# A Mamba-style mixer with a postnorm mixture layer on one core: per-bank waits, a split first expert input, an unrolled batch loop and a reordered start

## The chip, the cores and the metric

The kernel runs on one core of a Trainium2 chip. The metric is the device time of one execution in microseconds (us), median of several runs. Engines are named as in the profile: PE (matmul) and PEld (its weight loads), DVE, ACT, POOL, and SP, which only issues DMAs.

## The reference

For each of 16 sequences of 512 tokens with 128 features, one layer:

```python
# mixer (8 heads of 64, state 64)
z = x @ Wz;  ssm_in = x @ Win                    # 128 -> 256, 128 -> B, C, dt, X
delta = softplus(dt_raw + dt_bias)
h = exp(delta * -exp(A_log)) * h + X_t * delta * B_t ;  y_t = h @ C_t     # scan over time
y = y + D_param * X
out = (y * (silu(z) @ Wzg)) @ Wout
x = layernorm(x + out)
# mixture: three top-3-of-12 routers dw1, dw2, dw3 from x @ P_w.T @ U.T
h = gelu(sum_e dw1[:, e] * (x @ W1[e].T))        # 128 -> 512
y = sum_e dw2[:, e] * (h @ W2[e].T) + dw3 @ b2   # 512 -> 128
x = layernorm(x + y)
```

All data are float32. Matmuls over large operands are done as three products of a rounded high part and a low part (`mm3`, lines 229 to 231).

## The kernel before

**Tiling.** One batch is one sequence, held as 4 chunks of 128 tokens. All weights stay on chip, each as a high (`_hi`) and a low (`_lo`) part. PSUM has two banks for the mixer (`mix_bank`), four for the mixture (`exp_bank`, `hb[0..3]` in the code), one shared (`turn_bank`) and one with ones on the diagonal (`unit_bank`).

**Order of the work.** There is no scheduler: each engine runs its own instruction stream, all written by the same Python functions in one order, and semaphores (`wait`, `sig`) join them. `mixer_alone` sets up the weights, does the mixer of batch 0 and the front of batch 1's. Then comes `body` for batch b: it interleaves the mixer of b (PE: scores, `mix_zg`, `mix_states`, `mix_y`, `mix_out`) with the mixture of batch p = b-1 (`expert_in` for 12 experts, `expert_gelu`, `expert_out` for 4 chunks by 3 groups), and, near its end, starts the front of the next batch (`mix_x`, `mix_bc`, `mix_dt`, `mix_step`, `mix_z`, `mix_X`). `body` is written out for batch 1, is a hardware loop (`Fori`) over batches 2 to 14, and is written out again for 15. `mixture_alone` ends the program with the mixture of batch 15. In the loop every wait whose count depends on the batch is computed in a register.

**The first expert.** `expert_row` (L1021, DVE) multiplies the transposed input by a row of router weights into `fbuf`; `expert_split` rounds it on ACT into a slot of `sp_hi` (L1036), and POOL writes the remainder to `sp_lo` (L1039). The slots of `sp_hi` and `sp_lo` that expert 0 takes are, for the batch before, gelu outputs that `expert_out` reads until its last group. The four banks that expert 0 fills are the ones that DVE empties in the last four groups of `expert_out` (L1126, and L1129 adds the two accumulators). The code of the wait before is

```python
if e == 0:
    wait(PE, "comb", b.prev())
wait(PE, "xw_lo", b, e + 1)
```

**The gate and the step size.** `mix_z` computes z on PE, tanh on ACT (L599), and finishes silu on DVE (L602); its two results lie in the banks that `mix_X` needs next. `mix_step` is the softplus chain for delta: 16 small POOL operations (L530 to L557), with an exp (L517) and a log (L519) on ACT and a reciprocal on DVE (L522). Tanh and log are in different ACT tables, so that each change is an ACT_TABLE_LOAD.

**The start.** `split_w` makes the two parts of the weight tiles, k = 0 to 15 in a ring of four stages in `fbuf`, k = 16 to 23 from other buffers; the high part is made on ACT (L408), the low part on POOL or, for the k in `LO_V`, on DVE (L412). `load_w` on SP loads a stage again once its low part is done. For heads h, ACT scales the scores (L771), DVE adds the skip (L780) and scans the decay (L791), POOL multiplies both (L798, `Wt`), and PE forms y of a pair of heads (L816, L824). The router's path is x1 transposed (L919), logits (L932), twelve maxima and the rest of `route_weights` on DVE (L952 to L976), one transpose (L990), and two trips through DRAM that spread the rows.

## Time and profile before

| | us |
|---|---|
| median of 3 runs (range) | 1641.73 (1641.39 to 1641.86) |
| the profiled execution | 1642.74 |
| its span | 1641.0 |
| PE busy | 1565.2 (95%) |
| DVE busy | 1135.9 (69%) |
| ACT busy | 592.5 (36%) |
| POOL busy | 648.8 (40%) |
| granted TensorE clock, mean of the span | 0.982 |

The span is the profiled execution as its trace shows it; its own time is 1.74 us longer, for what lies around the trace. Busy times are sums over instructions; a busy engine is not thereby the one that sets the end. In a row of the timeline the first number is the start from the beginning of the span, the second the duration, both in us; the bracket at the end says how long the engine had been idle before it, and what ended that.

### The profile page before, as it was taken

The numbers are of one execution on the slowest core, as the hardware profiler recorded it, in microseconds if no ns is written. First come the engines' busy times: TensorE is split into PE (matmuls) and PEld (weight loads), VectorE is DVE, ScalarE is ACT, GpSimd is POOL, SyncE is SP. The second block draws the span as 40 slices with busy tenths as digits, with TensorE's granted clock in tenths as the row PEclk, the third lists the DMA queues.
The fourth block names the chain that finished last, engine by engine and source line by source line (L and its number), as shares of the span: only waits on it lengthen the run. The fifth ranks groups of instructions, "written<-read, shape, count | busy, mean of one in ns | idle before, by whom it ended". The sixth has DMA issues, their size and how long they took to land.

```text
span 1641.0 us, 28331 instructions
## 1 busy us (share of the span) xinstructions
PE 1565.2 (95%) x8466; PEld 1244.5 (76%) x8466; DVE 1135.9 (69%) x3110; ACT 592.5 (36%) x1339; POOL 648.8 (40%) x740
## 2 busy tenths in 40 slices
PE   6579999999999999999999999999999999999997
PEld 4457878787787878778787777877778787787776
DVE  6457677766867767677776768677687776767744
ACT  5443342424424243342424424242342414334130
POOL 4565260623516153351624526063351614435040
PEclk9679999999999999999999999999999999999999
DMA  4332140312304032140302304031130402213020
GB/s 139 113 100 75 38 119 27 104 45 63 93 27 129 13 95 67 44 112 20 120 29 68 88 27 128 17 105 53 55 100 25 131 13 82 80 45 112 19 67 7
DMA packets 81839, 114.63 MB, mean 70 GB/s; under 512 B 10176, under 2 KB 37328, under 8 KB 81744
## 3 DMA queue, kind: packets, MB, share of 16 engines
q1 hardware_dynamic: 81744, 113.71, 23.5%
q14 instruction: 78, 0.64, 0.2%
q8 instruction: 17, 0.28, 0.1%
HBM read 108.55 MB, written 5.13 MB: 69 GB/s over the span
## 4 chain that ended last, share of the span: by engine, by line
PE 75%; issue 8%; POOL 7%; DVE 5%; ACT 3%; DMA 1%; POOLq 0%; SPq 0%; DVEq 0%; ACTq 0%
PE exp_bank L229 19%; PE exp_bank L231 18%; PE exp_bank L230 18%; PE mix_bank L816 4%; PE mix_bank L842 4%; PE mix_bank L824 3%; POOL sp_lo L1039 3%; PE mix_bank L229 2%; PE mix_bank L231 2%; PE mix_bank L230 2%; ACT L515 1%; PE turn_bank L1087 1%; DVE Xd L626 1%; POOL Wt L798 1%; PE mix_bank L932 1%
## 5 line engine op out<-in xcount | busy, mean ns | idle before, releaser
L1039 POOL TENSOR_TENSOR sp_lo<-fbuf,sp_hi 128x512 fp32r<-128x512 f32 x192 | 247.6, 1290 | 260.8 <-ACT sp_hi L1036 246.4
L229 PE MATMUL exp_bank<-sp_hi,w_hi 128*128 128x512 f32 x768 | 311.8, 406 | 17.8 <-DVE acc L1129 15.0
L229 PE MATMUL exp_bank<-w_hi,sp_hi 128*128 128x512 f32 x768 | 309.7, 403 | 2.0 <-POOL sp_lo L1080 2.0
L231 PE MATMUL exp_bank<-sp_hi,w_lo 128*128 128x512 f32 x768 | 303.8, 396 | 0.0
L231 PE MATMUL exp_bank<-w_hi,sp_lo 128*128 128x512 f32 x768 | 303.3, 395 | 0.0
L230 PE MATMUL exp_bank<-w_lo,sp_hi 128*128 128x512 f32 x768 | 303.2, 395 | 0.0
L230 PE MATMUL exp_bank<-sp_lo,w_hi 128*128 128x512 f32 x768 | 302.1, 393 | 0.0
L1036 ACT CAST sp_hi<-fbuf 128x512 fp32r<-128x512 f32 x192 | 119.0, 620 | 373.9 <-DVE fbuf L1021 304.1
L1126 DVE SCALAR_TENSOR_TENSOR acc<-exp_bank,dw,acc 128x128 f32<-128x128 f32 x384 | 131.2, 342 | 126.9 <-PE exp_bank L231 126.0
L229 PEld LDWEIGHTS exp_bank<-sp_hi,w_hi 128*128 128x128 f32 x768 | 144.9, 189 | 68.2 <-POOL sp_lo L1039 22.5
L798 POOL TENSOR_TENSOR Wt<-Wt,Gh 128x512 f32<-128x512 f32 x128 | 175.4, 1370 | 11.3 <-DVE Wt L791 11.2
L530 POOL TENSOR_TENSOR delta<-delta,bias_b 128x32 f32<-128x32 f32 x16 | 4.3, 268 | 436.5 <-ACT delta L507 436.5
L229 PEld LDWEIGHTS exp_bank<-w_hi,sp_hi 128*128 128x128 f32 x768 | 144.3, 188 | 35.3 <-issue 2.0
L231 PEld LDWEIGHTS exp_bank<-w_hi,sp_lo 128*128 128x128 f32 x768 | 144.1, 188 | 35.0
L231 PEld LDWEIGHTS exp_bank<-sp_hi,w_lo 128*128 128x128 f32 x768 | 145.1, 189 | 32.1
L771 ACT ACTIVATE Gh<-Gm,delta 128x128 f32<-128x128 f32 x512 | 163.5, 390 | 15.9 <-POOL Wt L798 11.7
L230 PEld LDWEIGHTS exp_bank<-w_lo,sp_hi 128*128 128x128 f32 x768 | 144.4, 188 | 31.7
L230 PEld LDWEIGHTS exp_bank<-sp_lo,w_hi 128*128 128x128 f32 x768 | 145.1, 189 | 29.4
L791 DVE TENSOR_TENSOR_SCAN Wt<-seg_b,unit_bank 128x512 f32<-128x512 f32 x128 | 154.2, 1205 | 0.4 <-DMA seg_b<-dA_rows 0.4
L1021 DVE TENSOR_TENSOR fbuf<-turn_bank,row_b 128x512 f32<-128x512 f32 x192 | 129.7, 677 | 28.0 <-DMA row_b<-dw_rows 25.3
L1126 DVE SCALAR_TENSOR_TENSOR acc_odd<-exp_bank,dw,acc_odd 128x128 f32<-128x128 f32 x320 | 109.4, 342 | 1.5
L780 DVE SCALAR_TENSOR_TENSOR Gh<-unit_bank,d_b,Gh 128x512 f32<-128x512 f32 x128 | 94.4, 738 | 9.6 <-ACT Gh L771 9.6
(198 smaller groups left out, 2229.1 us busy)
## 6 DMA issues: line engine op xcount, KB each, us to landing
row_b<-dw_rows SPq DMA_DIRECT2D x192, 256.0 KB, 3.4
seg_b<-dA_rows SPq DMA_DIRECT2D x128, 256.0 KB, 3.7
ctd<-cum_rows SPq DMA_DIRECT2D x128, 96.0 KB, 3.4
x_in<-in_x SPq DMA_DIRECT2D x16, 256.0 KB, 2.8
result<-acc SPq DMA_DIRECT2D x16, 256.0 KB, 2.3
fbuf<-in_W1T SPq DMA_DIRECT2D x12, 256.0 KB, 3.4
fbuf<-in_W2T SPq DMA_DIRECT2D x4, 256.0 KB, 2.7
Gh<-in_W2T SPq DMA_DIRECT2D x4, 256.0 KB, 3.5
```

The source lines that it names most:

```text
L229: nc.tensor.matmul(ps, s_hi, m_hi, start=start and j == 0, stop=False)
L230: nc.tensor.matmul(ps, s_hi, m_lo, start=False, stop=False)
L231: last = nc.tensor.matmul(ps, s_lo, m_hi, start=False, stop=stop and j == n - 1)
L771: last = AC.activation(G[:, c, :], Gm[:, c, :], ACT.Copy, scale=delta[:, c, h:h + 1])
L780: sig("G_skip", DVE.scalar_tensor_tensor(flat, unit[:, :], d_b[:, h:h + 1], flat, ALU.mult, ALU.add))
L791: sig("scan", DVE.tensor_tensor_scan(W, seg_b[h % 2][:, :], unit[:, :], 0.0, ALU.mult, ALU.add))
L798: sig("W", PO.tensor_tensor(W, W, Gh[h % 2][:, :, :].rearrange("p c t -> p (c t)"), ALU.mult))
L816: PE.matmul(ps[j * HD:(j + 1) * HD, tok(c)], Xd[:, c, h * HD:(h + 1) * HD], Wt[:, q % 2, at:at + P], start=(c == 0), stop=False)
L1021: sig("xw", DVE.tensor_tensor(wide[e % 2], rb[:, :], row_b[e % 2][:, :], ALU.mult))
L1036: sig("xw_hi", AC.copy(sp_hi[:, at, :], wide[e % 2]))
L1039: sig("xw_lo", PO.tensor_tensor(sp_lo[:, at, :], wide[e % 2], sp_hi[:, at, :].bitcast(F32), ALU.subtract))
L1126: sig("comb", DVE.scalar_tensor_tensor(dst, ps, w, dst, ALU.mult, ALU.add))
```

## The change

1. `expert_in`: expert 0 waits, bank by bank, for the group of `expert_out` that used this bank, and not for all of the batch before.
2. `expert_split` for expert 0 works in two pieces: tokens of chunks 0 to 2 (384 columns) once the groups of chunks 0 to 2 of `expert_out` are through, and chunk 3 (128 columns) after the last group. The first piece is issued at the end of the body, with `expert_row` ahead of it, and the second at the start of the next one.
3. At the end of the body `mix_step` stands ahead of `mix_z`, without a table load of its own; the load for exp and log follows the two tanh.
4. The loop is gone: `body` is written out for batches 2 to 14, so that all waits are against constants.
5. The start: `setup_zg` is taken apart, its ACT part after `mix_dt`, its DVE part after the first silu split; `LO_V` is (0, 1), so that tiles 3 and 5 have their low part on POOL; the splits of tiles 2 to 15 are spread otherwise; `mix_from_start` follows `mix_decay`; the front of batch 1 is interleaved with the router in another order, with its `Xd` copies on ACT and not DVE.

```diff
             xw=E, xw_hi=E + 1, xw_lo=E + 1, ps_h=E - 1, ...
-        N1, NHP, LO_V = 16, 2, (0, 1, 3, 5)
+        N1, NHP, LO_V = 16, 2, (0, 1)
...
-        def expert_split(eng, b, e):
+        def expert_split(eng, b, e, parts=(0, 1)):
             at = (e + 2) % NH
-            if eng is AC:
-                wait(AC, "xw", b, e + 1)
-                wait(AC, "ps_y", b.prev())
...
+            early = slice(0, (NC - 1) * P)
+            pieces = ((1, early), (2, tok(NC - 1))) if e == 0 else ((e + 2, slice(0, T)),)
+            for k, (n, cols) in enumerate(pieces):
+                if k not in parts:
+                    continue
+                if eng is AC:
+                    wait(AC, "xw", b, e + 1)
+                    wait(AC, "ps_y", b.prev(), (NC - 1) * NG if cols == early else None)
...
+                    sig("xw_hi", AC.copy(sp_hi[:, at, cols], wide[e % 2][:, cols]))
...
         def expert_in(eng, b, e):
-                if e == 0:
-                    wait(PE, "comb", b.prev())
-                wait(PE, "xw_lo", b, e + 1)
+                wait(PE, "xw_lo", b, e + 2)
                 for hc in range(NH):
+                    if e == 0:
+                        m = NC * NG - NH + hc
+                        wait(PE, "comb", b.prev(), m // NG * (E + 1) + (m % NG + 1) * EG)
...
         def body(eng, b, front_next, norm_before=True):
             if norm_before:
-                expert_split(eng, p, 0)
+                expert_split(eng, p, 0, [1])
...
             if front_next:
+                mix_step(eng, nxt, table=False)
                 mix_z(eng, nxt)
-                mix_step(eng, nxt)
+                if eng is AC:
+                    AC.preload_act_table_set(LOG_EXP)
+            expert_row(eng, b, 0)
+            expert_split(eng, b, 0, [0])
             expert_out(eng, p, 3, range(1, NG - 1))
-            expert_row(eng, b, 0)
...
         def mixer_alone(eng, b):
-            setup_zg(eng)
+            setup_masks(eng)
             mix_bc(eng, b)
             mix_dt(eng, b)
+            if eng is AC:
+                setup_zg(eng)
...
             mix_silu_split(eng, b, on=DVE)
+            if eng is DVE:
+                setup_zg(eng)
...
-            split_w(eng, range(2, 6))
             router_product(eng)
             mix_states(eng, b)
+            split_w(eng, range(2, 4))
             mix_decay(eng, b, 0)
             mix_decay(eng, b, 1)
+            split_w(eng, [4])
             mix_zg(eng, b, range(0, 2))
             mix_score_step(eng, b, 2)
             mix_zg(eng, b, range(2, 4))
-            split_w(eng, range(6, 8))
+            mix_from_start(eng, b, 0)
...
-                split_w(eng, [k])
-                k += 1
+                split_w(eng, [k, k + 1])
+                k += 2
...
             route_transpose(eng, b)
+            mix_step(eng, nxt)
+            mix_z(eng, nxt)
             route_logits(eng, b)
+            mix_silu_split(eng, nxt)
+            mix_X(eng, nxt, [0, 1], on=AC)
+            route_weights(eng, b)
+            mix_scores(eng, nxt)
+            if eng is not SP:
+                mix_rates(eng, nxt)
+            if eng in (PE, AC):
+                mix_ends(eng, nxt)
+            mix_X(eng, nxt, [2], on=AC)
             split_w(eng, range(N1, N1 + LATE))
+            if eng is PO:
+                mix_ends(eng, nxt)
+            route_rows(eng, b)
...
         def program(eng):
-            waited[id(eng)] = {}
-            with eng.Fori(2, NB - 1) as i:
-                body(eng, Batch(i, 0), True)
-            waited[id(eng)] = {}
+            for i in range(2, NB - 1):
+                body(eng, Batch(None, i), True)
```

ACT at the end of a pass of the loop and the start of the next, before. L507 is the copy of dt_raw, L599 tanh, L515, L517 and L519 the table load, exp and log of the step size; L1388 is the loop, and the row behind it is the first of the pass.

```order
L507 COPY delta<-mix_bank 128x32
L203 REGISTER_ALU
L599 ACT_TABLE_LOAD
L599 ACTIVATE Wt<-mix_bank 128x512
L203 REGISTER_ALU
L599 ACTIVATE Wt<-mix_bank 128x512
L515 ACT_TABLE_LOAD
L203 ISA
L517 ACTIVATE dt_s<-dt_s 128x32
L203 REGISTER_ALU
L519 ACTIVATE dt_s<-dt_s 128x32
L1388 COMPARE_AND_BRANCH
```

And in the change, where L602 is tanh, L1261 the table load behind it, and L1051 the two pieces of the first expert's input.

```order
L510 COPY delta<-mix_bank 128x32
L520 ACTIVATE dt_s<-dt_s 128x32
L522 ACTIVATE dt_s<-dt_s 128x32
L602 ACT_TABLE_LOAD
L602 ACTIVATE Wt<-mix_bank 128x512 x2
L1261 ACT_TABLE_LOAD
L1051 CAST sp_hi<-fbuf 128x384
L1051 CAST sp_hi<-fbuf 128x128
L704 COPY Gm<-mix_bank 128x512
```

Exp and log come first, tanh behind them and behind a table load; the number of table loads is the same, and the branch and register rows are gone.

POOL in the mixer of batch 0, before. L726 is the last work ahead of the heads, L412 the low part of a weight tile, L798 the product of a head.

```order
L726 TENSOR_TENSOR Wt<-Xd,ends 128x512 x3
L412 TENSOR_TENSOR w1_lo<-fbuf,w1_hi 128x512 x2
L798 TENSOR_TENSOR Wt<-Wt,Gh0 128x512
L798 TENSOR_TENSOR Wt<-Wt,Gh1 128x512
L412 TENSOR_TENSOR w1_lo<-fbuf,w1_hi 128x512 x2
L798 TENSOR_TENSOR Wt<-Wt,Gh0 128x512
L412 TENSOR_TENSOR w1_lo<-fbuf,w1_hi 128x512
L798 TENSOR_TENSOR Wt<-Wt,Gh1 128x512
```

And in the change, with L735, L415 and L807 for the same.

```order
L735 TENSOR_TENSOR Wt<-Xd,ends 128x512 x3
L415 TENSOR_TENSOR w1_lo<-fbuf,w1_hi 128x512 x2
L807 TENSOR_TENSOR Wt<-Wt,Gh0 128x512
L807 TENSOR_TENSOR Wt<-Wt,Gh1 128x512
L415 TENSOR_TENSOR w1_lo<-fbuf,w1_hi 128x512
L807 TENSOR_TENSOR Wt<-Wt,Gh0 128x512
L415 TENSOR_TENSOR w1_lo<-fbuf,w1_hi 128x512 x2
L807 TENSOR_TENSOR Wt<-Wt,Gh1 128x512
```

The product of head 2 has one tile ahead of it and not two, that of head 3 two and not one.

PE in the front of batch 1, before: z (its last product), then the transpose of the router weights (L990), then X0, X1 and the scores.

```order
L231 MATMUL mix_bank<-xT_hi,wz_lo 128x512
L990 MATMUL exp_bank<-ident,dwpad 128x128
L229 MATMUL mix_bank<-wx_hi,xT_hi 128x512
L230 MATMUL mix_bank<-wx_lo,xT_hi 128x512
L231 MATMUL mix_bank<-wx_hi,xT_lo 128x512
```

And in the change: the transpose (L999) stands behind X0, X1, the scores, the rates and X2, right ahead of the gate's product.

```order
L714 MATMUL mix_bank<-a_rows,upper 128x32
L229 MATMUL mix_bank<-wx_hi,xT_hi 128x512
L230 MATMUL mix_bank<-wx_lo,xT_hi 128x512
L231 MATMUL mix_bank<-wx_hi,xT_lo 128x512
L999 MATMUL exp_bank<-ident,dwpad 128x128
L229 MATMUL mix_bank<-sp_hi,wzg_hi 128x512
```

## Rows read from the trace of the kernel before

**Rows 1.** The page, its first part: busy us (share of span) and instructions.

```profile
PE 1565.2 (95%) x8466; PEld 1244.5 (76%) x8466; DVE 1135.9 (69%) x3110; ACT 592.5 (36%) x1339; POOL 648.8 (40%) x740
```

**Rows 2.** The timeline of PE: the first expert's first matmul in four batches.

```profile
199.24 0.50 PE L229 MATMUL exp_bank<-sp_hi,w_hi 128*128 128x512 f32 x1 [0.91 <-DVE acc L1129]
...
295.96 0.49 PE L229 MATMUL exp_bank<-sp_hi,w_hi 128*128 128x512 f32 x1 [0.92 <-DVE acc L1129]
...
1468.29 0.51 PE L229 MATMUL exp_bank<-sp_hi,w_hi 128*128 128x512 f32 x1 [0.90 <-DVE acc L1129]
...
1560.08 0.50 PE L229 MATMUL exp_bank<-sp_hi,w_hi 128*128 128x512 f32 x1 [2.25 <-DVE acc L1129]
```

**Rows 3.** The timeline of DVE and PE: after entering the loop, and after a jump.

```profile
199.90 0.82 DVE L658 TENSOR_TENSOR_SCAN cum_t<-dA_t,upper 32x128 f32<-32x128 f32 x1 [0.79 <-ACT dA_t L654]
...
591.76 1.27 DVE L658 TENSOR_TENSOR_SCAN cum_t<-dA_t,upper 32x128 f32<-32x128 f32 x1 [3.09 <-DMA dA_rows<-dA_t]
...
594.26 0.51 PE L229 MATMUL mix_bank<-sp_hi,wzg_hi 128*128 128x512 f32 x1 [0.34 <-DVE Xd L626]
```

**Rows 4.** DMA queues of 107 to 296 us: packets, MB, share of 16 engines.

```profile
q8 instruction: 8, 0.13, 0.3%
```

**Rows 5.** The timeline around the start of a pass, ACT, POOL, DVE and PE.

```profile
586.56 0.62 ACT L1036 CAST sp_hi<-fbuf 128x512 fp32r<-128x512 f32 x1 [4.12 <-PE exp_bank L231]
...
587.25 1.27 POOL L1039 TENSOR_TENSOR sp_lo<-fbuf,sp_hi 128x512 fp32r<-128x512 f32 x1 [0.16 <-ACT sp_hi L1036]
...
587.81 0.86 DVE L1129 TENSOR_TENSOR acc<-acc,acc_odd 128x128 f32<-128x128 f32 x1
...
588.80 0.50 PE L229 MATMUL exp_bank<-sp_hi,w_hi 128*128 128x512 f32 x1 [0.92 <-DVE acc L1129]
```

**Rows 6.** The timeline of ACT: a copy of 128 columns.

```profile
1160.19 0.27 ACT L995 COPY rows<-mix_bank 128x128 f32<-128x128 f32 x1 [3.52 <-PE mix_bank L990]
```

**Rows 7.** The timeline of the step size and the gate, in the order of starts.

```profile
578.12 0.25 POOL L535 TENSOR_TENSOR dt_s<-dt_s,delta 128x32 f32<-128x32 f32 x1
...
578.88 1.30 ACT L599 ACTIVATE Wt<-mix_bank 128x512 f32<-128x512 f32 x2 [0.84 <-PE mix_bank L231]
...
579.51 1.39 DVE L602 SCALAR_TENSOR_TENSOR Wt<-Wt,mix_bank 128x512 f32<-128x512 f32 x2
...
580.20 1.28 ACT L515 ACT_TABLE_LOAD   x1
...
581.49 0.23 ACT L517 ACTIVATE dt_s<-dt_s 128x32 f32<-128x32 f32 x1
...
582.17 0.40 PE L229 MATMUL mix_bank<-wx_hi,xT_hi 128*128 128x512 f32 x1
...
582.21 0.23 ACT L519 ACTIVATE dt_s<-dt_s 128x32 f32<-128x32 f32 x1 [0.49 <-POOL dt_s L539]
```

**Rows 8.** The timeline of the start, DVE, PE and POOL, batch 0.

```profile
26.68 3.49 DVE L412 TENSOR_TENSOR w_lo<-fbuf,w_hi 128x512 fp32r<-128x512 f32 x2 [0.28 <-ACT w_hi L408]
...
31.67 0.47 PE L229 MATMUL mix_bank<-sp_hi,wzg_hi 128*128 128x512 f32 x1 [4.26 <-DVE S L759]
...
40.22 2.56 POOL L412 TENSOR_TENSOR w_lo<-fbuf,w_hi 128x512 fp32r<-128x512 f32 x2 [3.67 <-ACT w_hi L408]
...
61.23 1.98 PE L816 MATMUL mix_bank<-Wt,Xd 128*64 128x128 f32 x16 [3.71 <-POOL Wt L798]
```

**Rows 9.** The timeline of DVE and PE: front of batch 1; then PE near the end.

```profile
83.63 0.97 DVE L952 MAX8 fbuf<-fbuf 128x8 f32<-128x12 f32 x12 [1.37 <-ACT fbuf L939]
...
92.93 0.45 PE L990 MATMUL exp_bank<-ident,dwpad 128*128 128x128 f32 x1 [7.00 <-issue]
...
99.17 0.39 PE L229 MATMUL mix_bank<-sp_hi,wzg_hi 128*128 128x512 f32 x1
...
107.22 0.50 PE L229 MATMUL exp_bank<-sp_hi,w_hi 128*128 128x512 f32 x1
...
1561.67 0.63 PE L229 MATMUL exp_bank<-sp_hi,w_hi 128*128 128x512 f32 x1
```

More of the change, by code:

```diff
@@ L329, in setup_z, with setup_masks @@
                 PE.wait_ge(sems["wbdt"], 2)
[L331 to L334 removed]
+        def setup_masks(eng):
             if eng is DVE:
@@ L340, in setup_zg @@
                 DVE.tensor_copy(unit[:, :], ident4[:, :]).then_inc(sems["cast"], 1)
+                DVE.wait_ge(sems["decay_par"], 48)
+        def setup_zg(eng):
+            if eng is AC:
+                AC.wait_ge(sems["wzg"], 16)
+                AC.activation(wzg_hi[:, :, :], st_wzg, ACT.Copy, scale=0.5).then_inc(sems["wzg_hi"], 1)
+            if eng is DVE:
                 DVE.wait_ge(sems["wzg_hi"], 1)
@@ L615, in mix_silu_split, with mix_X @@
                                                     ALU.subtract))
-        def mix_X(eng, b, cs):
+        def mix_X(eng, b, cs, on=DVE):
             for c in cs:
@@ L622, in mix_X @@
                     sig("ps_X", mm3(ps[:, :], [(xT_hi[:, tok(c)], xT_lo[:, tok(c)], wx_hi[:, :], wx_lo[:, :])]))
-                if eng is DVE:
-                    wait(DVE, "ps_X", b, c + 1)
-                    wait(DVE, "ps_yq", b.prev())
-                    sig("Xd", DVE.tensor_copy(Xd[:, c, :], bank_of(f"X{c}")[:, :]))
+                if eng is on:
+                    wait(on, "ps_X", b, c + 1)
+                    wait(on, "ps_yq", b.prev())
+                    sig("Xd", (AC.copy if on is AC else DVE.tensor_copy)(Xd[:, c, :], bank_of(f"X{c}")[:, :]))
         def mix_zg(eng, b, ns=range(NQ)):
@@ L642, in layer_program, with mix_rates @@
         R1 = slice(0, H * NC)
-        def mix_rates(eng, b):
+        def mix_rates(eng, b, start=True):
             if eng is PE:
@@ L669, in mix_rates, with start_rows @@
                 seg_row(b, 1)
+                if start:
+                    start_rows(eng, b)
+        def start_rows(eng, b):
+            if eng is SP:
                 start_row(b, 0)
@@ L1018, in expert_row @@
                 if e >= 2:
-                    wait(DVE, "xw_hi", b, e - 1)
-                    wait(DVE, "xw_lo", b, e - 1)
+                    wait(DVE, "xw_hi", b, e)
+                    wait(DVE, "xw_lo", b, e)
                 sig("xw", DVE.tensor_tensor(wide[e % 2], rb[:, :], row_b[e % 2][:, :], ALU.mult))
@@ L1024, in expert_row @@
                 expert_weight(b, e + 2)
-        def expert_split(eng, b, e):
+        def expert_split(eng, b, e, parts=(0, 1)):
             at = (e + 2) % NH
-            if eng is AC:
-                wait(AC, "xw", b, e + 1)
-                wait(AC, "ps_y", b.prev())
-                if e >= 4:
-                    wait(AC, "ps_h", b, e - 3)
-                elif e >= 2 and (b.reg is not None or b.off < NB - 1):
-                    wait(AC, "ps_zg", Batch(b.reg, b.off + 1))
-                sig("xw_hi", AC.copy(sp_hi[:, at, :], wide[e % 2]))
-            if eng is PO:
-                wait(PO, "xw_hi", b, e + 1)
-                sig("xw_lo", PO.tensor_tensor(sp_lo[:, at, :], wide[e % 2], sp_hi[:, at, :].bitcast(F32), ALU.subtract))
+            early = slice(0, (NC - 1) * P)
[6 more added lines that the diff above has]
+                    wait(AC, "ps_y", b.prev(), (NC - 1) * NG if cols == early else None)
+                    if e >= 4:
+                        wait(AC, "ps_h", b, e - 3)
+                    elif e >= 2 and (b.reg is not None or b.off < NB - 1):
+                        wait(AC, "ps_zg", Batch(b.reg, b.off + 1))
+                    sig("xw_hi", AC.copy(sp_hi[:, at, cols], wide[e % 2][:, cols]))
+                if eng is PO:
+                    wait(PO, "xw_hi", b, n)
+                    sig("xw_lo", PO.tensor_tensor(sp_lo[:, at, cols], wide[e % 2][:, cols],
+                                                  sp_hi[:, at, cols].bitcast(F32), ALU.subtract))
         def expert_in(eng, b, e):
@@ L1263, in mixer_alone @@
             mix_silu_split(eng, b, on=DVE)
+            if eng is DVE:
+                setup_zg(eng)
             if eng is AC:
```

44 lines of the change are left out of this document (14 added, 30 removed).

## The prediction

> **What bounds the kernel now.** I read the page first: PE is busy 95% of the span [rows 1]. The timeline of PE then says where the missing 5% is. From the first expert of batch 1 to the end it streams: in the middle of the program 128x512 matmuls follow each other without a gap, and only two idle rows return in every pass: about 0.9 us before the first expert [rows 2] and about 0.35 us before the gate's product [rows 3]. The reader should see in both that PE is the bound of the steady part, so that a microsecond taken from PE's waits there is a microsecond of the total, and that work of other engines counts only through these waits. The first 107 us are different: PE waits for POOL, DVE and the router for many microseconds [rows 8, 9]. So I cost four places: the jump, the boundary of the batches, the last boundary, and the start.
>
> **The jump of the loop (12 times).** Batch 2 enters the loop without a jump; the next 12 passes come after one. From first expert to first expert, batch 2 takes 295.96 - 199.24 = 96.72 us, and the 12 later passes (1468.29 - 295.96) / 12 = 97.69 us [rows 2]. The code is the same. What differs is seen on DVE: at a jump its first instruction comes 3.09 us after the one before, and without it 0.79 us [rows 3]. The profile puts those 3.09 us down to a DMA, but nothing in the code makes this scan wait for it, and it happens exactly where there is a jump; I take it to be the fetch of code behind the branch. The late scan makes the copy of X2 late, and PE waits 0.34 us for it [rows 3]; the rest of the 0.97 us comes later in the pass, through expert inputs that are late by the same cause. Unrolled, all passes should run as batch 2: -12 x 0.97 = **-11.7 us**. The registers cost nothing that I can see: batch 2 computes them too, and DVE, ACT and POOL have slack. Bounds: 0 if the fetch stall is not the jump's, and the full 11.7.
>
> The Trainium skill (Runtime: NRT & Kernel Launch, Instruction fetch mechanics) says that prefetch of code is sequential, and that a taken branch outside the current window forces a fetch before execution goes on. The 3.09 against 0.79 us agree with it.
>
> The price of unrolling is more code to fetch. In 107 to 296 us, nearly all straight code, the queue that carries PE's code moved 8 packets [rows 4], about 4 per batch, and those matmuls ran with no gap beyond those named. I charge nothing.
>
> **The boundary (14 times).** Now PE goes on at 588.80, having been idle for 0.92 us, so it was free at 587.88 [rows 5]. Two chains end together: POOL's low part at 587.25 + 1.27 = 588.52, and DVE's last add at 587.81 + 0.86 = 588.67. The change removes the second: bank 0 was emptied long before, and the last bank needs the last multiply, which ends before the add at 587.81 starts, while PE comes to it nine matmuls after its start. It shortens the first: behind the last group ACT and POOL handle 128 columns and not 512. For ACT the nearest row is a 128x128 copy, 0.27 us [rows 6]. For POOL, 128x32 takes 0.25 and 128x512 takes 1.27 [rows 5, 7]; linear between them is 0.46. Chain: 586.56 + 0.27 + 0.07 (587.25 against the end of ACT's piece) + 0.46 = 587.36, plus 0.13 (588.67 to 588.80) = 587.49, ahead of PE's 587.88. So the whole 0.92 goes. Even with POOL at 0.85 us, the wait is gone. The 384-column piece runs while PE works on the last two groups; DVE makes its row before the combines of the second-last group, which it did before those of the last one until now.
>
> What is late next? First, the gate. Exp and log now go first: POOL's fourth step ends at 578.37 [rows 7], exp can start at about 578.4, log starts 0.72 after exp as now (582.21 against 581.49) and takes 0.23, so ACT is free at about 579.35. Table load 1.28, tanh 0.65 each (1.30 for two): the first ends at 581.3, silu (1.39 for two, so 0.7) at 582.0. X0 needs that bank at 582.17, and its weights 0.23 earlier. I charge 0.15 us. Second, the gate's low part on POOL does not move with the boundary, since ACT makes the high part behind the scores: zg comes 0.92 earlier and should wait about 0.1. So the boundary gives 0.92 - 0.25 = 0.67 us, 14 times: **-9.4 us**. Bounds: 0 if another wait takes the place, 0.92 x 14 = -12.9 at most.
>
> Here a rule speaks against the change. The row says that exp starts 0.01 us after the load of 1.28 us has ended [rows 7], so that a change of tables costs 1.28. The Trainium skill (ScalarE: Activation LUTs, What ACT_TABLE_LOAD costs) adds a drain of about 1380 ns, 2.66 us in all. By it tanh would be 1.38 us later, and X0 would stall for some 1.5 us in every pass, so that the boundary would lose 0.6 us and not gain 0.67. The row shows no drain; I go by the row.
>
> **The last boundary (once).** PE was idle for 2.25 us before 1560.08 [rows 2], with ACT, POOL at full width and DVE behind each other. The short chain saves 0.35 + 0.81 us, and the add is not waited for: -1.2. Behind this gap eight matmuls ran at the lower clock (1.2 GHz; 0.63 us each, the first at 1561.67 [rows 9], against 0.40), each some 0.2 us longer from start to start; behind the 14 gaps of 0.92 none did. With a gap of about 1.1 the clock should stay up: -1.6. Together **-2.8 us** (bounds -1.2 and -2.8).
>
> **The start (once).** I followed the order by hand with the durations of the trace. Against: PE's rates wait for the low part of Wzg, which DVE now makes behind the silu split, some 1.2 us later than PE is ready. For: DVE loses two weight tiles of 3.49 us that stood ahead of the states, for which PE waited 4.26 us at the gate [rows 8]; net the gate starts some 1.7 us earlier. Then PE waits ahead of each later pair of heads for POOL's products, at the last for 3.71 us [rows 8]. POOL had two tiles, 2.56 us, ahead of head 2 [rows 8], and SP loaded rows behind waits for such tiles. With one tile ahead of head 2 and two ahead of heads 3, 5 and 7 I get the products of heads 3, 5 and 7 ready at about 43.6, 49.3 and 55.9, and y3 at 56 and not 61.2: -5.2. POOL has two tiles more, which end near 62, in time for the first expert weights. In the front of batch 1, PE stood for 7.00 us before the transposed router weights at 92.93 [rows 9], with X0 to X2 behind it until 99.17, 5.7 us of work. Those now go first; but DVE makes silu ahead of the maxima, which puts the maxima 1.6 us later than 83.63 (I get 85.2), and part of the gate's product will run at the lower clock, 1.5 us: -5.7 + 1.6 + 1.5 = -2.6. What batch 1 waits for behind its first expert stays. Start: **-7.8 us**, bounds -2 and -12.
>
> **Sum.** -11.7 - 9.4 - 2.8 - 7.8 = -31.7. The profiled execution took 1642.74 (span 1641.0), which gives 1611.0; it stood 1.0 us above the median of the runs, so I predict 1610 us.
>
> **The rivals.**
> - *Tanh is late.* A drain, or a later log, and every pass waits at X0. For it: the chain above has under 0.2 us to spare. Against: the load row. With 1.3 us more in 14 passes: 1610 + 18 = 1628. Chance 0.07.
> - *The start gives nothing.* My hand order leaves out queues of DMAs and has POOL fuller than before. Then 1618. For it: POOL's two more tiles and the late Wzg; against: the waits of 7.00 and 3.71 us [rows 8, 9]. Chance 0.12.
> - *The boundary doesn't move.* The change does not do what it says there: another wait, for the piece on POOL behind a slow ACT, takes the place of the one removed: 1610 + 9 = 1619. Against it are the 0.4 us to spare. Chance 0.08.
> - *Code does not arrive (slower).* Unrolled, PE fetches about 4 blocks in each of 12 more batches, 50 in all, and on the other engines the stream never repeats. If each block stalled PE for the 2.3 us that DVE lost at a jump (3.09 - 0.79), that is +115, less the gain of 32: 1725. It decides from 32 / 50 = 0.65 us per block on. Against it: batch 2 fetched the same way without a gap [rows 4]. Chance 0.02.
>
> **How the numbers follow.** The forecast has 0.71. Its own range is the sum's with the start between -2 and -12 and the boundary between 0.3 and 0.9 us: about 1603 to 1620. Taking in the first three rivals gives 1601 to 1625. Faster by over 0.2% (3.3 us, about what a measurement of this kernel tells from no change) holds in all cases but the last: 0.97, the same 0.01, slower 0.02.
>
> **What would show it.** Right: DVE's scan at every boundary idle for about 0.8 us; no idle row before the gate's product; the first expert with no wait, or under 0.2; pass after pass of 95.9 to 96.2 us between first experts; the first expert of batch 1 at about 99.4 and not 107.2. Wrong: an idle row before X0 with DVE's silu as its releaser (the gate is late), "issue" rows of PE at irregular places (code), or y3 still at 61 us. If passes are 95.2 us, the charge of 0.25 was too much.

## The result, and the profile after

The changed kernel takes 1606.59 us (median of 4 runs, 1604.72 to 1607.62), the kernel before on the same chip 1641.8. The ratio is 0.9783 with a 95% interval of 0.9766 to 0.98: 2.2% faster. I had predicted 1610 us with a range of 1601 to 1625, so the time lies 3.4 us below the forecast and within its range. Three of the four terms that make the sum were too small, though, and one of them for a reason that the prediction did not see. The four together were to give 31.7 us; the spans of the two profiled executions differ by 37.1. That the median lies closer to the forecast is in part luck: the profiled execution before was 1.0 us above its median, for which I allowed, and the one after is 0.55 us below its own.

| | before | after |
|---|---|---|
| median us | 1641.8 | 1606.59 |
| profiled execution, its span | 1642.74, 1641.0 | 1606.04, 1603.9 |
| first expert of batch 1 starts | 107.22 | 98.39 |
| from there to the last boundary but one (1468.29, 1433.93) | 1361.07 | 1335.54 |
| from there to the end | 172.71 | 169.97 |
| a pass in the middle, mean | 97.69 | 95.74 |

The three stretches give 8.83 + 25.53 + 2.74 = 37.1 us, the difference of the spans. The page of the profile after shows in its first part, its queues and the chain of work that ended last (by engine):

```profile
PE 1556.4 (97%) x8466; PEld 1242.3 (77%) x8466; DVE 1098.5 (68%) x3104; ACT 596.9 (37%) x1359; POOL 653.5 (41%) x758
...
q8 instruction: 67, 1.10, 0.3%
q14 instruction: 59, 0.48, 0.1%
...
PE 94%; POOL 2%; ACT 1%; DVE 1%; DMA 1%; issue 1%; SPq 0%; POOLq 0%; ACTq 0%; DVEq 0%
```

PE has 9 us less of busy time than in [rows 1], but its share rose to 97%. The unrolled program fetches PE's code in 67 packets (queue q8), where the kernel before needed 17, and no "issue" row of PE stands behind the first expert of batch 1. The other queue with code (q14) has 59 packets where the loop had 78. The timeline of PE, which answers to [rows 2], shows that the boundary has lost its idle row:

```profile
98.39 0.47 PE L229 MATMUL exp_bank<-sp_hi,w_hi 128*128 128x512 f32 x1 [0.99 <-POOL sp_lo L1054]
...
189.30 0.48 PE L229 MATMUL exp_bank<-sp_hi,w_hi 128*128 128x512 f32 x1
...
285.01 0.48 PE L229 MATMUL exp_bank<-sp_hi,w_hi 128*128 128x512 f32 x1
...
380.49 0.39 PE L714 MATMUL mix_bank<-a_rows,upper 128*128 128x32 f32 x2
380.71 0.48 PE L229 MATMUL exp_bank<-sp_hi,w_hi 128*128 128x512 f32 x1
...
1524.54 0.50 PE L229 MATMUL exp_bank<-sp_hi,w_hi 128*128 128x512 f32 x1 [0.92 <-POOL sp_lo L1054]
```

The pair of short matmuls before the first expert (L714) now starts 0.22 us ahead of it, two steps of 0.11 us with no idle time; before it was 1.30 us. The last boundary waits 0.92 us and not 2.25. The timeline of ACT, POOL and DVE around that boundary, which answers to [rows 5]:

```profile
376.19 0.52 ACT L1051 CAST sp_hi<-fbuf 128x384 fp32r<-128x384 f32 x1 [0.17 <-DVE fbuf L1030]
...
379.55 0.30 ACT L1051 CAST sp_hi<-fbuf 128x128 fp32r<-128x128 f32 x1 [2.84 <-PE exp_bank L231]
...
376.88 1.02 POOL L1054 TENSOR_TENSOR sp_lo<-fbuf,sp_hi 128x384 fp32r<-128x384 f32 x1
...
379.92 0.46 POOL L1054 TENSOR_TENSOR sp_lo<-fbuf,sp_hi 128x128 fp32r<-128x128 f32 x1 [2.03 <-ACT sp_hi L1051]
...
380.71 0.29 DVE L1146 TENSOR_TENSOR acc<-acc,acc_odd 128x128 f32<-128x128 f32 x1
382.31 0.89 DVE L661 TENSOR_TENSOR_SCAN cum_t<-dA_t,upper 32x128 f32<-32x128 f32 x1 [1.31 <-ACT dA_t L657]
```

POOL's last piece takes 0.46 us, as estimated. The surprise is DVE's add: 0.29 us, where the same instruction took 0.86 in [rows 5]. What differs is that POOL was in its 1.27 us instruction then, and now rests (its last piece ended at 380.38). And ACT with DVE and PE ahead of it, which answers to [rows 7]:

```profile
372.10 0.23 ACT L522 ACTIVATE dt_s<-dt_s 128x32 f32<-128x32 f32 x1 [0.49 <-POOL dt_s L542]
372.34 1.28 ACT L602 ACT_TABLE_LOAD   x1
373.64 1.09 ACT L602 ACTIVATE Wt<-mix_bank 128x512 f32<-128x512 f32 x2
...
374.27 1.29 DVE L605 SCALAR_TENSOR_TENSOR Wt<-Wt,mix_bank 128x512 f32<-128x512 f32 x2 [0.52 <-ACT Wt L602]
...
375.15 0.39 PE L229 MATMUL mix_bank<-wx_hi,xT_hi 128*128 128x512 f32 x1
```

The load takes 1.28 us and tanh starts 0.02 us behind its end; X0 (the last row) follows with no idle time. By the rule of the Trainium skill (ScalarE: Activation LUTs, What ACT_TABLE_LOAD costs) a drain would have come on top; the trace shows none in this place.

### The profile page after: what moved, and what is told of

Read it like the earlier page. It is cut to its first block, busy times and chain, and to the rows that moved or that the text cites. A ratio compares the mean times of both kernels' runs of the same rounds, so it can differ in the third digit from the quotient of the medians.

```text
span 1603.9 us, 24955 instructions
## 1 busy us (share of the span) xinstructions
PE 1556.4 (97%) x8466; PEld 1242.3 (77%) x8466; DVE 1098.5 (68%) x3104; ACT 596.9 (37%) x1359; POOL 653.5 (41%) x758
## 4 chain that ended last, share of the span: by engine, by line
PE 94%; POOL 2%; ACT 1%; DVE 1%; DMA 1%; issue 1%; SPq 0%; POOLq 0%; ACTq 0%; DVEq 0%
PE exp_bank L229 23%; PE exp_bank L231 22%; PE exp_bank L230 22%; PE mix_bank L825 4%; PE mix_bank L851 4%; PE mix_bank L229 4%; PE mix_bank L231 3%; PE mix_bank L230 3%; PE mix_bank L833 3%; PE mix_bank L751 1%; PE mix_bank L699 1%; PE turn_bank L1104 1%; POOL w_lo L415 1%; PE mix_bank L941 1%; PE mix_bank L500 1%
## 5 line engine op out<-in xcount | busy, mean ns | idle before, releaser
L1054 POOL TENSOR_TENSOR sp_lo<-fbuf,sp_hi 128x512 fp32r<-128x512 f32 (+2 forms) x208 | 249.6, 1204 | 258.6 <-ACT sp_hi L1051 140.5
L229 PE MATMUL exp_bank<-sp_hi,w_hi 128*128 128x512 f32 x768 | 308.5, 402 | 4.4 <-POOL sp_lo L1054 4.4
L1051 ACT CAST sp_hi<-fbuf 128x512 fp32r<-128x512 f32 (+2 forms) x208 | 121.9, 588 | 311.6 <-DVE fbuf L1030 269.6
L807 POOL TENSOR_TENSOR Wt<-Wt,Gh 128x512 f32<-128x512 f32 x128 | 175.8, 1374 | 6.9 <-DVE Wt L800 6.7
L231 PEld LDWEIGHTS exp_bank<-sp_hi,w_lo 128*128 128x128 f32 x768 | 144.6, 188 | 30.9
L230 PEld LDWEIGHTS exp_bank<-sp_lo,w_hi 128*128 128x128 f32 x768 | 144.8, 189 | 30.3
```

The source lines that it names most:

```text
L229: nc.tensor.matmul(ps, s_hi, m_hi, start=start and j == 0, stop=False)
L230: nc.tensor.matmul(ps, s_hi, m_lo, start=False, stop=False)
L231: last = nc.tensor.matmul(ps, s_lo, m_hi, start=False, stop=stop and j == n - 1)
L807: sig("W", PO.tensor_tensor(W, W, Gh[h % 2][:, :, :].rearrange("p c t -> p (c t)"), ALU.mult))
L1051: sig("xw_hi", AC.copy(sp_hi[:, at, cols], wide[e % 2][:, cols]))
L1054: sig("xw_lo", PO.tensor_tensor(sp_lo[:, at, cols], wide[e % 2][:, cols], sp_hi[:, at, cols].bitcast(F32), ALU.subtract))
```

## The experiments

Each kernel ran beside the kernel before on the same chip. The difference to the changed kernel is given by the ratios to the kernel before, times 1641.7; an interval of a ratio is 0.0013 to 0.0017 to each side, 2 to 3 us, and that of a difference of two ratios is wider. "Pass" is the mean from first expert to first expert in the profiled run, over the 13 passes from the second boundary to the last but one (with the loop restored, the 12 behind a jump). "Gap" is the start of the first expert less that of the pair of matmuls before it (L714 in the changed kernel), in a pass of the middle.

| kernel | median us | ratio | against after | pass | gap |
|---|---|---|---|---|---|
| the changed kernel again | 1605.25 | 0.9783 | 0 | 95.74 | 0.22 |
| loop restored | 1613.8 | 0.9829 | +7.6 | 96.56 | 0.22 |
| one wait for all banks | 1607.62 | 0.9795 | +2.0 | 95.91 | 0.56 |
| input in one piece | 1617.43 | 0.9848 | +10.7 | 96.48 | 1.13 |
| gate first | 1614.33 | 0.9836 | +8.7 | 96.33 | 1.00 |
| old start | 1615.17 | 0.9841 | +9.5 | 95.72 | 0.22 |
| old first routing only | 1609.55 | 0.9792 | +1.5 | 95.71 | 0.22 |
| load on POOL | 1609.31 | 0.9802 | +3.1 | 95.75 | 0.22 |
| before, loop written out | 1627.76 | 0.992 | (-13.1 to before) | 96.58 | 1.28 |
| silu rounded first | 1604.77 | 0.9762 | -3.4 | 95.56 | 0.22 |
| one tile later | 1604.81 | 0.9771 | -2.0 | 95.73 | 0.22 |
| both | 1601.75 | 0.9755 | -4.6 | 95.53 | 0.22 |

**The changed kernel again.**

> The changed kernel once more, as the base of the runs beside it: 1606.6 us within 1.5, if the result is repeatable. The rows to compare with: DVE's first addition at the first expert 0.29 us, passes of 95.7 us, DVE's scan at the turn of the batch idle for 1.31 us for its input from ScalarE.

It gave 1605.25 us (1604.09 to 1607.94) at the same ratio, with the same passes. Its runs spread over nearly 4 us, and the traces of kernels with the same start show where: the last wait for POOL's product (y3) ends at 55.1 to 59.0 us in them, with the granted clock at its lower level in other stretches each time, while the middle repeats to some 0.2 us a pass. A second place is the pass of batch 1. In most traces the clock is at its lower level once more for 3.4 us, between 108 and 125 us, and from the first expert of batch 1 to that of batch 2 it is 90.9 to 93.5 us; in three (one wait, load on POOL, both) it is not, and it is 89.2 to 89.7 us. So the start can't be read from one trace to better than 1 to 2 us.

**The loop.**

```diff
-            for i in range(2, NB - 1):
-                body(eng, Batch(None, i), True)
+            with eng.Fori(2, NB - 1) as i:
+                body(eng, Batch(i, 0), True)
```

> Only the loop is restored: 12 passes jump back again, all else is the changed kernel. Theory (each jump costs about 0.97 us on DVE's way to PE): 11.7 us slower, about 1618.3 us, each pass from the second to the last 96.7 instead of 95.7 us, and the idle time ahead of DVE's scan back at about 3 us. Rival (the time came off the boundary alone, and the jump was covered): within 1 us of the changed kernel. A second rival (code written out costs something that the jump saved, as more packets of the instruction queues): faster than the changed kernel.

By the medians 8.6 us slower, by the ratios 7.6; the spans of the two traces differ by 11.0. So the jump costs time as I said, and somewhat less behind the new boundary (12 x 0.82 = 9.8 us by the passes). Against the straight kernel, PE loses it at two places of a pass, in batch 4's for one: at the gate's product 5 us into it (0.39 us) and at an expert input 22 us into it (0.37 us). DVE's scan, with the loop:

```profile
385.79 0.41 DVE L661 TENSOR_TENSOR_SCAN cum_t<-dA_t,upper 32x128 f32<-32x128 f32 x1 [3.33 <-DMA dA_rows<-dA_t]
```

The profile blames a DMA again, and the idle time goes with the jump again: the loop is the only thing that was changed. That it is the jump and not the registers of the loop's code shows in batch 2, which runs the same code without a jump ahead of it: its scan is idle for 1.45 us against 1.31 straight, and its pass takes 95.82 us. The packets of code say what happens at a jump. From 284 to 1440 us PE's queue (q8) moves none in this trace, and q14 moves 60 packets of 8 KB, five in every pass; in all 12 passes behind a jump, three of the five start 0.7, 1.5 to 1.6 and 4.1 to 4.5 us after the first expert. In the straight kernel q14's packets lie scattered, and 10 of 13 boundaries have none in this stretch. So code is fetched at each jump, for engines other than PE. That it is what DVE waits for fits, but isn't shown, since the trace doesn't say which engine a packet is for. The rival that the written-out code costs something is out.

The first pass behind a jump takes 97.64 us and the later ones 96.2 to 96.7, and the rows of DVE and POOL show why:

```profile
288.45 1.30 DVE L661 TENSOR_TENSOR_SCAN cum_t<-dA_t,upper 32x128 f32<-32x128 f32 x1 [3.64 <-DMA dA_rows<-dA_t]
...
288.44 2.16 POOL L735 TENSOR_TENSOR Wt<-Xd,ends 128x512 f32<-128x512 f32 x2 [0.28 <-POOL ends L729]
...
290.99 0.50 PE L229 MATMUL mix_bank<-sp_hi,wzg_hi 128*128 128x512 f32 x1 [1.30 <-DVE Xd L629]
```

There the scan begins together with a long instruction of POOL and takes 1.30 us; in the 11 later passes it falls ahead of POOL's and takes 0.41.

**The same edit on the kernel before.** Its loop written out, all else as before.

```diff
-            with eng.Fori(2, NB - 1) as i:
-                body(eng, Batch(i, 0), True)
+            for i in range(2, NB - 1):
+                body(eng, Batch(None, i), True)
```

> The kernel before, with nothing but its loop written out. Theory (the jump is worth the same with the old boundary as with the new): 8.5 to 11 us faster than the kernel before, 1631 to 1633 us, passes of 96.8 us instead of 97.7, DVE's scan idle 1.3 instead of 3.1 us. Rival (the long wait at the first expert covered a part of the jump): 3 to 6 us faster.

It is faster than I expected, 13.4 us by the medians, and passes take 96.58 us, 1.11 less than 97.69. The scan behind the turn, the add before it and the first expert now read:

```profile
584.87 0.88 DVE L658 TENSOR_TENSOR_SCAN cum_t<-dA_t,upper 32x128 f32<-32x128 f32 x1 [0.59 <-ACT dA_t L654]
...
583.27 1.00 DVE L1129 TENSOR_TENSOR acc<-acc,acc_odd 128x128 f32<-128x128 f32 x1
...
584.33 0.50 PE L229 MATMUL exp_bank<-sp_hi,w_hi 128*128 128x512 f32 x1 [0.89 <-DVE acc L1129]
```

So the rival that the old boundary covered a part of the jump falls, and the reverse holds: with the old boundary the jump costs more. A likely reason, not tried alone, is in the same rows as above: in the kernel before all 12 scans behind a jump take 1.07 to 1.28 us beside POOL, and with the new boundary 11 of 12 take 0.41. A straight pass takes 0.14 us less than batch 2 of the kernel before (96.72), which enters the loop. Its scan has 0.59 us of idle time ahead of it and batch 2's has 0.79 [rows 3], but that is not where the 0.14 arises: on PE the two passes run alike until 81 us into them, where batch 2 is 0.09 us late at the first product of `mix_bc`. Why is not known.

**One wait for all banks.**

```diff
+                if e == 0:
+                    wait(PE, "comb", b.prev())
...
-                    if e == 0:
-                        m = NC * NG - NH + hc
-                        wait(PE, "comb", b.prev(), m // NG * (E + 1) + (m % NG + 1) * EG)
```

> The first expert's first multiply waits for the whole of the last weighted output again, instead of one bank at a time. In the changed kernel DVE's last addition before it takes 0.29 us and ends 0.29 us after PE has started, in the kernel before it took 0.86 us. Theory A (the addition was slow there because POOL worked at the same time on its low part of 512 columns; the split has ended that, the wait itself is worth only what the addition lasts): PE starts 0.3 to 0.45 us later at each of 15 boundaries, so 4 to 7 us slower, and the addition still takes about 0.3 us. Rival B (my forecast's reading, the wait was worth the whole stop): 0.92 us at each of 14 boundaries, 13 us slower. Rival C (PE is held by something else there): no change.

It is slower by 2.0 us by the ratios and 2.4 by the medians, less than A said (4 to 7) and far from B. The runs alone could not tell this from no change (C); the gap and the passes do. The gap is 0.34 us longer, as A had it, and the add still takes 0.29 us, but a pass is only 0.17 us longer. Where the rest goes is seen 3.6 us into a pass: there the changed kernel has a stop ahead of the gate's first product, which waits for low parts that POOL ends at 384.29; it costs 0.17 to 0.19 us, and it disappears when PE comes later. In the changed kernel:

```profile
383.55 0.40 PE L229 MATMUL mix_bank<-wx_hi,xT_hi 128*128 128x512 f32 x1
...
384.35 0.50 PE L229 MATMUL mix_bank<-sp_hi,wzg_hi 128*128 128x512 f32 x1
...
381.62 2.67 POOL L617 TENSOR_TENSOR sp_lo<-Wt,sp_hi 128x512 fp32r<-128x512 f32 x2 [1.24 <-ACT sp_hi L614]
```

From X2 to the gate's product it is 0.80 us for three matmuls that start 0.23 us apart, and the second matmul there starts 0.34 us behind the first.

**The input in one piece.** The counts of the waits are changed to match, which is left out here.

```diff
-            pieces = ((1, early), (2, tok(NC - 1))) if e == 0 else ((e + 2, slice(0, T)),)
+            pieces = (None, (1, slice(0, T))) if e == 0 else ((e + 1, slice(0, T)),)
```

> The first expert's input is made in one piece of 512 columns again, behind its last transpose; the wait by banks stays. Theory (PE is then held by the low part, which POOL makes in about 1.3 us instead of 0.46, and not by DVE's addition): about 0.9 us more at each of 14 or 15 boundaries, 13 to 15 us slower, a wait for the low part of about 0.9 us ahead of the first expert, and DVE's addition beside it at 0.8 to 0.9 us instead of 0.29, if POOL's longer instruction is what slows it. Rival (the bank wait alone brought the gain at the boundary): within 2 us of the changed kernel. For the slow addition there is a rival too: if it depends on what it waits for and not on POOL, it stays at 0.3 us.

It is slower by 10.7 us by the ratios, less than the 13 to 15 expected; the gap is 0.91 us longer and a pass 0.74, since the stop at the gate is absorbed again. So the split is the part of the boundary that matters. The chip also answers the question of the slow add. The timeline of DVE and POOL in this kernel:

```profile
382.18 1.00 DVE L1147 TENSOR_TENSOR acc<-acc,acc_odd 128x128 f32<-128x128 f32 x1
...
381.77 1.27 POOL L1055 TENSOR_TENSOR sp_lo<-fbuf,sp_hi 128x512 fp32r<-128x512 f32 x1 [3.35 <-ACT sp_hi L1052]
```

POOL ends at 383.04 and the add at 383.18. Of DVE's, nothing but the counts of two waits was edited, and 0.29 became 1.00.

**Load on POOL.** Three products that nobody reads, put where POOL has nothing to do in the first routing. Their targets are the state tiles, which are dead there.

```diff
+            if eng is PO:
+                for to, n in ((S[:, 0:2, :].rearrange("p c n -> p (c n)"), T), (S[:, 2, :], T // 2), (St[:, :], T // 2)):
+                    PO.tensor_tensor(to, wx_hi[:, 0:n].bitcast(F32), wx_lo[:, 0:n].bitcast(F32), ALU.subtract)
```

> POOL computes three products that nobody reads (one of 128x512 and two of 128x256, about 2.5 us in all) in a gap of 3.2 us that it has in the first routing, while DVE works on the router. Nothing waits for them, and POOL's next own work comes 3.2 us after the gap's start. Theory (POOL's and DVE's instructions on on-chip memory hold each other up): DVE's instructions of 128x144 beside them take up to POOL's whole instruction, so that the router ends 1 to 2.5 us later and the first expert of the second batch starts up to 2 us later. Rival (DVE's long instructions in the kernel before had another cause): DVE's rows stay within 0.05 us of the changed kernel's (three of 128x144 in 0.74 us) and the time stays.

The timeline of DVE in the router, first the changed kernel with the transposed router weights on PE, then the one with the load, with POOL's rows:

```profile
83.88 1.23 DVE L967 TENSOR_TENSOR fbuf<-fbuf 128x144 f32<-128x144 f32 x1
85.15 0.74 DVE L970 TENSOR_TENSOR fbuf<-iota_e,ix 128x144 f32<-128x144 f32 x3
...
88.15 0.30 PE L999 MATMUL exp_bank<-ident,dwpad 128*128 128x128 f32 x1 [1.18 <-issue]
```

```profile
85.53 2.77 DVE L970 TENSOR_TENSOR fbuf<-iota_e,ix 128x144 f32<-128x144 f32 x3
88.33 0.31 DVE L973 TENSOR_TENSOR fbuf<-fbuf 128x144 f32<-128x144 f32 x1
88.67 1.33 DVE L974 TENSOR_TENSOR fbuf<-fbuf 128x144 f32<-128x144 f32 x1
90.03 1.25 DVE L976 TENSOR_TENSOR fbuf<-fbuf 128x144 f32<-128x144 f32 x1
...
85.28 2.10 POOL L1356 TENSOR_TENSOR S<-wx_hi,wx_lo 128x512 f32<-128x512 f32 x2
87.34 0.79 POOL L1356 TENSOR_TENSOR St<-wx_hi,wx_lo 128x256 f32<-128x256 f32 x1
88.56 2.56 POOL L415 TENSOR_TENSOR w_lo<-Gh,w_hi 128x512 fp32r<-128x512 f32 x2 [0.43 <-ACT w_hi L411]
```

The three of L970 take 2.77 us and not 0.74, while POOL is at the load; those behind them run at 0.31 us where POOL is idle (88.13 to 88.56) and at 1.25 to 1.33 beside POOL's next low parts, which in the changed kernel begin only when the router is done. The transposed router weights come to PE 25.5 us after the output's transposes (94.02 against 68.51) and not 20.0, so 2.9 us of idle POOL time filled made the router 5.5 us later, more than I had expected (1 to 2.5), and the first expert of batch 1 6.4 us later behind the output's transposes (up to 2 expected). Only 2.0 us of it stand beside the load itself; the rest comes because the router, once late, runs into POOL's next work. The median is 3 to 4 us slower. The effect is shown, with the other engine's load as the only edit.

**Gate first.**

```diff
-                mix_step(eng, nxt, table=False)
...
-                if eng is AC:
-                    AC.preload_act_table_set(LOG_EXP)
+                mix_step(eng, nxt)
```

> The gate's tanh goes ahead of the step size chain again, in every batch; loop, pieces and waits stay as changed. In the changed kernel POOL ends the chain 3.8 us before the first expert's first multiply, and makes the early piece's low part (1.02 us) right behind it. Theory (the split needs the chain early): POOL's chain ends some 3.3 us later, the early piece is queued behind it, and the first expert waits 0.8 to 1.2 us for its low part at 14 boundaries: 11 to 16 us slower than the changed kernel's 1605.3, so the gain of the split is gone. Rival (the order on ScalarE matters little, since POOL has time): within 2 us. Second rival (the tanh was late in the changed kernel and held the next batch's X): faster by 1 to 2 us.

The mechanism is as written, the size is below the range (8.7 us by the ratios, 11 to 16 expected): POOL's chain ends at 381.80, 1.47 us ahead of the first expert at 383.27, and both pieces follow it.

```profile
381.54 0.26 POOL L560 TENSOR_TENSOR a_lo<-a_rows,a_hi 128x32 fp32r<-128x32 f32 x1
381.76 1.46 POOL L1054 TENSOR_TENSOR sp_lo<-fbuf,sp_hi 128x384 fp32r<-128x384 f32 x2
```

The gap is 0.78 us longer and the pass 0.59: the 0.19 at the gate's product is absorbed here too, which my expectation left out. This shows what the order of tables is for: it clears POOL for the split.

**Old start, and the old first routing alone.** The orders of the first batch's mixer and of the first routing, in full or the second alone, are put back as in the kernel before. The core of the two edits, first the start, then the routing:

```diff
-        N1, NHP, LO_V = 16, 2, (0, 1)
+        N1, NHP, LO_V = 16, 2, (0, 1, 3, 5)
...
-            if eng is DVE:
-                setup_zg(eng)
...
+            split_w(eng, range(2, 6))
             router_product(eng)
             mix_states(eng, b)
-            split_w(eng, range(2, 4))
```

```diff
+            split_w(eng, range(N1, N1 + LATE))
...
+            route_weights(eng, b)
+            route_rows(eng, b)
...
             mix_silu_split(eng, nxt)
-            mix_X(eng, nxt, [0, 1], on=AC)
-            route_weights(eng, b)
+            mix_X(eng, nxt, [0, 1])
             mix_scores(eng, nxt)
```

> The order of the start and of the first routing is as in the kernel before, the rest is the changed kernel. Theory (the parts add up): the first expert of the second batch starts at 107 instead of 98.4 us and the whole is 8.8 us slower, about 1614. Rival (the time won at the start is partly won by the other parts, as the split): 5 to 7 us slower. DVE's instruction for the rank of the router's choices takes 3.8 us again beside POOL's low part of the weights, if the two hold each other up.

> Only the order of the first routing, beside the front of the second batch, is as in the kernel before; the start of the first batch stays as changed. The old order of both cost 9.9 us (1615.2 against 1605.3). Theory by the traces (start 4.1, front 4.7): 4 to 6 us slower than the changed kernel, with DVE's three instructions of 128x144 at 3.8 us beside POOL's low parts of the weights. Rival (by my forecast's sizes, front 2.6 and start 5.2): 2 to 3 us slower.

Both together cost 9.5 us by the ratios against 8.8 expected: the sum holds. In the trace of the full one, DVE's three instructions take 3.82 us beside POOL's low parts:

```profile
87.97 3.82 DVE L967 TENSOR_TENSOR fbuf<-iota_e,ix 128x144 f32<-128x144 f32 x3
...
86.49 2.58 POOL L412 TENSOR_TENSOR w_lo<-Gh,w_hi 128x512 fp32r<-128x512 f32 x2
89.02 2.61 POOL L412 TENSOR_TENSOR w_lo<-seg_b,w_hi 128x512 fp32r<-128x512 f32 x2
```

For the old routing alone the runs do not settle the size: 1607.3 to 1612.7 us, by the ratios 1.5 us slower, with an interval of over 3 us around that, which is below the 4 to 6 expected. The traces do: from the transposes of the output to the first expert of batch 1 it is 35.2 us with the old routing, 35.0 with the old start, and 30.2 to 30.3 in the six kernels with the new order and no edit of the start or the routing.

**Two moves that the traces suggested.** ScalarE rounds silu ahead of copying the scores; and of the two weight tiles that POOL splits ahead of head 7's decay, one goes behind it.

```diff
+                if eng is AC:
+                    mix_silu_split(eng, b)
                 mix_scores(eng, b)
-                mix_silu_split(eng, b)
+                if eng is not AC:
+                    mix_silu_split(eng, b)
```

```diff
-                split_w(eng, [k, k + 1])
-                k += 2
+                n = (2, 2, 1, 3)[q]
+                split_w(eng, range(k, k + n))
+                k += n
```

> The changed kernel with one more move: ScalarE rounds the silu of the next batch ahead of copying the scores, so that POOL starts its low part some 0.5 us earlier. In the changed kernel the multiply with the gate's weights stands still 0.09 us for this low part 3.6 us into a pass, and the next one comes 0.10 us late as well. Theory (this stop is on PE's path and POOL's late start is its cause): 0.19 us less in each of 14 passes, 2.7 us faster than the changed kernel, passes of 95.53 us. Rival (the copied scores come 1.1 us later and their next user becomes late): slower, with a new wait after the first expert. Second rival (the stop has another cause): the same time and the step of 3.64 us in place.

> The changed kernel with one more move at the start: one of the two weight tiles that POOL splits ahead of the decay of head 7 is split behind it. There POOL's low parts end 1.5 us after DVE's scan of head 7, and the last y of the first batch waits for POOL. Theory: the product for head 7 comes 1.2 to 1.5 us earlier, and with it the last y, the output, the routing and the first expert of the second batch, so about 1.3 us faster. Rival (what is moved back is late for the stages behind it, since the ring of four stages is freed later): 0 to 2 us slower.

> Both moves at once. Theory (one works in the passes, the other at the start, and they share nothing): the gains add up to about 4 us, 1601 to 1602 us. Rival: less than the larger of the two alone.

The first takes 0.18 us from a pass, as expected. In the trace of the second, the last y comes 1.3 us sooner: from the one before it to it 5.39 us and not 6.68. In the kernel with both:

```profile
51.22 1.36 PE L825 MATMUL mix_bank<-Wt,Xd 128*64 128x128 f32 x16 [2.55 <-POOL Wt L807]
...
56.60 1.97 PE L825 MATMUL mix_bank<-Wt,Xd 128*64 128x128 f32 x16 [2.55 <-POOL Wt L807]
```

Both at once give 1601.75 us (1601.34 to 1604.39), ratio 0.9755 (0.9741 to 0.9768): 4.6 us below the changed kernel by the ratios. Its interval only just reaches that of the changed kernel (0.9766 to 0.98), so the sign is likely. Of its size, the traces carry the part of the passes, 14 x 0.18 to 0.21 = 2.5 to 2.9 us. What the 1.3 us at the last y leave further on is open: from the output's transposes to the first expert it is 30.9 and 30.5 us with this move and not 30.2 to 30.3, and the first expert of batch 1 starts at 94.27 in one trace and 98.24 in the other, against 96.14 and 98.39 in those of the changed kernel. The runs can't tell either move alone from no change.

## Why the prediction was right, and where its terms were off

**The jump.** Right in kind: idle time behind the branch, with no code that waits for the DMA named, and packets of code at each jump; that DVE waits for them is likely and not shown. Predicted 11.7, measured 13.4 on the kernel before (13.3 by 12 passes of 1.11 us; the interval of the ratio is 10.5 to 15.9 us, so the runs alone don't refute 11.7). The step that was off is "Unrolled, all passes should run as batch 2": a straight pass takes 96.58 and not 96.72. Undone on the changed kernel it is worth 8 to 10 us; the two parts share some of their gain, so which one is given more depends on the order in which they are made.

**The boundary.** Predicted 0.67 us a pass, measured 96.58 - 95.74 = 0.84, so 11.8 us for 14 and not 9.4. The whole stop went, as forecast, and it was worth more than its idle row of 0.92: the gap fell by 1.06 us (1.28 to 0.22), since the second matmul behind a stop starts 0.34 us after the first and not 0.23. The charge of 0.15 for X0 was wrong: silu's first half ends at 374.96, 0.19 us ahead of X0 at 375.15. The charge of 0.1 for the gate's low part was right in place, and it is 0.19 in all, as taking it away showed. That gives 1.06 - 0.19 = 0.87, close to the 0.84. That two chains end together was right too: the wait by banks is worth 0.1 us a pass without the split (one piece against the kernel before, both without the loop: 96.48 against 96.58) and 0.17 with it, the split without the wait 0.67 (95.91), both 0.84. What I had not seen is that one chain is long because of the other: the add's 0.86 us was POOL's doing.

**The last boundary.** Predicted 2.8, measured 2.74: the gap is 0.92 and the clock behind it stays at its upper level.

**The start.** Predicted 7.8, measured 8.83. The first batch: 5.2 predicted, 4.1 in the one trace, 4.5 by the means over the traces of either order (three old, nine new), which themselves spread over 2.1 and 4.4 us. The routing: 2.6 predicted, 4.7 measured, and here the step that failed can be named. I had the maxima 1.6 us later, and they are 1.5 us later (12.86 and 11.38 us behind the output's transposes). I had 5.7 - 1.5 = 4.2 us for the work that now goes ahead of PE's wait, and it is 4.05. What is missing is that the router behind the maxima became 2.2 us shorter: its instructions of 128x144 took 3.82 and 0.31 us (L961 and L958), and now take 0.74 and 1.23 (L970 and L967), since POOL's low parts of the weights begin when it has ended.

**The rivals.** Tanh is not late: no drain, X0 without an idle row. The start gives nearly nine us. The boundary moves by all that it could. Code arrives: 67 packets in place of 17, with no "issue" rows beyond those of the start.

**The signs.** Two that I had named came out beside their range: passes take 95.74 us and not 95.9 to 96.2, for the sizes given above, and DVE's scan is idle for 1.31 us and not 0.8. I had carried the 0.8 over from the old boundary; PE doesn't wait for it.

## What to carry over

When an instruction takes several times longer in one place than its twin elsewhere, look at what the neighbour engine does in the same microsecond before taking the duration as its price; work that "fills an idle engine" can delay the engine beside it by more than its own length. A loop's jump can stop an engine (here DVE, for over 3 us each time), and shows as an idle row with an unrelated releaser; where code size allows it, write the loop out. And price a removed wait by the pass, not by the gap: here the next wait took back 0.17 to 0.19 us each time.

## What the runs showed of the hardware

DVE and POOL hold each other up on SBUF. DVE's add of two SBUF tiles takes 0.29 us alone, 0.86 to 1.00 beside POOL's 1.27 us instruction, and ends 0.14 us after it; three instructions of 128x144 take 0.74 us alone and 2.77 to 3.82 beside POOL. In the kernel before, the 15 adds beside POOL take 0.86 to 1.00 and the 49 others 0.29. POOL is held too: its product of a head (L807) takes 1.29 us, and mostly 1.61 where DVE is in L814 (two SBUF operands) at its start. One operand alone can be held too: DVE's rounding of the gelu output (L1091), which reads one tile of SBUF, takes 0.43 us alone and up to 1.52 beside POOL. Instructions with an operand in PSUM are not held: in the changed kernel's start, beside a low part that POOL works at from 40.62 to 43.53, one reads

```profile
42.91 0.74 DVE L789 SCALAR_TENSOR_TENSOR Gh<-unit_bank,d_b,Gh 128x512 f32<-128x512 f32 x1
```

and all 128 of this line take 0.73 to 0.75, of which 82 run beside POOL. The Trainium skill (SBUF — State Buffer, SBUF: two separate sides) has a rule for this: DVE's second pair of ports is shared with GpSimd and locked for a whole instruction, which a DVE instruction with two SBUF inputs meets. The traces agree with it: the add ends 0.14 us behind POOL's instruction, and one with a PSUM operand is spared. The prediction did not weigh it. Moving an operand of the slow add to PSUM was not tried.

The table load of ACT ahead of tanh takes 1.28 us in each pass of the changed kernel; the activation before it ends at most 0.02 us ahead, and tanh starts at most 0.02 us behind.
